# Gate logarithms, their chunk totals and the column-tiled products of a gated linear-attention and ternary feed-forward layer on Trainium2

## The reference

```python
xn = layernorm(x)
Q, K, V = xn @ Wq.T, xn @ Wk.T, xn @ Wv.T            # per head 16 wide
g     = max(sigmoid(xn_head @ gw.T), 1e-6)
log_c = clip(cumsum(log(g), axis=tokens), -30, 30)   # per head
Gc    = exp(log_c) + 1e-6
R     = silu(K @ sw.T)
S     = cumsum(K V^T * R / Gc, axis=tokens) * Gc     # a 16x16 state per head
attn  = (Q S) @ Wo.T
h     = bitlinear(xn, w_fc) + gate * (xn @ v.T @ fast_b.T @ u.T)    # ternary weights, 1024 hidden
ffn   = bitlinear(relu(h) ** 2, w_proj)
out   = x + attn + ffn
```

## Time and profile before

| | before |
|---|---|
| median of 3 runs | 652.83 us |
| profiled execution | 652.83 us |
| span of its profile | 651.0 us |
| PE busy | 629.2 us, 97% of the span |
| DVE, ACT, POOL busy | 507.5, 435.3, 357.1 us |
| granted TensorE clock, mean | 0.998 |
| chain that ended last | PE 92%, DMA 3%, SP queue 2% |

### The profile page before, as it was taken

One profiled execution on the slowest core, in us unless ns is written; L12 is line 12 of the kernel. 1 busy time (PEld: TensorE's weight loads), 2 busy tenths in 40 slices (PEclk: granted clock), 3 DMA queues, 4 the chain that ended last, 5 costly groups with the idle time before them and its releaser, 6 DMA issues.

```text
span 651.0 us, 21292 instructions
## 1 busy us (share of the span) xinstructions
PE 629.2 (97%) x7734; PEld 546.5 (84%) x7734; DVE 507.5 (78%) x1245; ACT 435.3 (67%) x999; POOL 357.1 (55%) x434
## 2 busy tenths in 40 slices
PE   3889999999999999999999999999999999999997
PEld 3668888888888888888888888888888888888886
DVE  5998888878787777877778877877787777878673
ACT  2688666767666776766677676667676666767662
POOL 4766465554555555456455555645555554655355
PEclk9999999999999999999999999999999999999999
DMA  9347755666746765554567856667656465677421
GB/s 309 94 124 121 111 140 135 148 142 131 111 117 129 138 132 139 135 119 112 130 139 136 143 130 97 132 136 129 143 130 135 106 125 128 141 128 127 100 45 34
DMA packets 186793, 83.05 MB, mean 128 GB/s; under 512 B 118320, under 2 KB 186160, under 8 KB 186688
## 3 DMA queue, kind: packets, MB, share of 16 engines
q1 hardware_dynamic: 184448, 79.05, 58.3%
q10 hardware_dynamic: 2240, 2.62, 1.2%
HBM read 12.43 MB, written 8.39 MB: 32 GB/s over the span
## 4 chain that ended last, share of the span: by engine, by line
PE 92%; DMA 3%; SPq 2%; DVE 1%; issue 1%; POOL 0%; POOLq 0%; DVEq 0%
PE y_bank L2251 17%; PE attn_bank L2195 9%; PE hid_b L2230 9%; PE hid_a L2230 9%; PE front_b L2132 7%; PE y_bank L2265 7%; PE front_a L2113 6%; PE front_b L2094 6%; PE score_a L2161 5%; PE attn_bank L2209 5%; PE score_b L2161 4%; PE attn_bank L2180 3%; PE hid_a L2232 2%; PE hid_b L2232 2%; DMA x_sb<-in_x 2%
## 5 line engine op out<-in xcount | busy, mean ns | idle before, releaser
L2251 PE MATMUL y_bank<-wproj_t,sq_h 128*128 128x256 f16 x512 | 118.5, 273 | 0.0
L2251 PE MATMUL y_bank<-wproj_t,sq_l 128*128 128x256 f16 x512 | 118.5, 273 | 0.0
L1727 DVE TENSOR_TENSOR sq_l<-relu_sq,sq_h 128x512 f16<-128x512 f32 x128 | 105.3, 824 | 1.0 <-ACT relu_sq L1032 0.9
L1680 DVE TENSOR_TENSOR masked<-score_a,shapes_sb 128x512 f32<-128x512 f32 x128 | 87.0, 680 | 16.0 <-PE score_a L2161 15.9
L1680 DVE TENSOR_TENSOR masked<-score_b,shapes_sb 128x512 f32<-128x512 f32 x128 | 87.2, 681 | 11.8 <-PE score_b L2161 11.7
L666 POOL TENSOR_TENSOR state_diag<-state,state_mask 128x256 f32<-128x256 f32 x56 | 53.4, 954 | 63.6 <-DVE state L1699 63.1
L1032 ACT ACTIVATE relu_sq<-relu_sq 128x512 f32<-128x512 f32 x128 | 79.6, 623 | 9.8 <-DVE sq_l L1727 9.7
L653 POOL COPY decay_halves<-decay 128x1024 uint16<-128x1024 uint16 x32 | 33.2, 1038 | 87.3 <-ACT decay L983 87.3
L697 POOL TENSOR_TENSOR y_both<-y_both,x_sb 128x512 f32<-128x512 f32 x32 | 41.2, 1287 | 70.0 <-DVE y_both L1739 70.0
L1023 ACT ACTIVATE sq_h<-relu_sq 128x512 f16<-128x512 f32 x128 | 79.2, 620 | 0.1
L933 ACT ACTIVATE vg<-front_b 128x304 f32<-128x304 f32 x64 | 27.2, 425 | 71.9 <-PE front_b L2132 71.8
(11 more groups left out here) (189 smaller groups left out, 1662.2 us busy)
## 6 DMA issues: line engine op xcount, KB each, us to landing
q_diag<-q SPq DMA_DIRECT2D x256, 64.0 KB, 2.7
k_stack<-k SPq DMA_DIRECT2D x128, 128.0 KB, 3.8
x_sb<-in_x SPq DMA_DIRECT2D x32, 256.0 KB, 3.3
out_y<-y_both SPq DMA_DIRECT2D x32, 256.0 KB, 3.4
relu_sq<-in_w_fc ACTq DMA_DIRECT2D x1, 1024.0 KB, 11.1
pj_nat<-in_w_proj ACTq DMA_DIRECT2D x1, 1024.0 KB, 13.8
y_both<-in_w_qk ACTq DMA_DIRECT2D x1, 512.0 KB, 4.6
w_stage<-in_w_qkvz_t SPq DMA_DIRECT2D x1, 512.0 KB, 6.3
```

The lines of the kernel that those rows point to most:

```text
L1680: nc.vector.tensor_tensor(masked[:, c, g].rearrange("p (h n) -> p h n", h=4), score_bank[g % 2][:].rearrange("p (h n) -> p h n", h=4), cau ...
L1727: nc.vector.tensor_tensor(sq_l[:, q], sq[:, n], sq_h[:, q], ALU.subtract).then_inc(sq_l_done, 1)
L2251: last = mm(y_bank[:, c * D:(c + 1) * D], part[:, q, at:at + P], wproj_t[:, 2 * q + i], start=(q == i == c == n == 0), stop=False, skip_gr ...
```

## The change

Seven things change.
1. The running sum is one fp16 product of 64 columns. The logarithm, times 1024, is taken as two fp16 parts (`log_high` on ACT, `log_low` on DVE); the sum of what stood before is no longer in the product.
2. DVE adds the two parts out of front_a at once (`sums_taken`), which frees that bank; `keys` waits for it and no longer for `clip_log`. The last row of that result, the totals of the two chunks, is copied from partition 127 to all partitions by a transfer of SP (`spread_totals`), and POOL adds them up (`sums_before`). `clip_log` becomes two instructions.
3. The two chunks' `values` and both `state_updates` stand in one block; the updates go to the second score bank, the values of both chunks to the four quarters of attn_bank. `chunk_out` (twice, 256 elements) becomes `unit_out` (once, 512).
4. `scores` (c, g) = (0, 1) waits until the state has been read out of that bank. `diagonal_state` waits for `carried` instead of DVE.
5. DVE's two small `tensor_scalar` in `dens` become `scalar_tensor_tensor` with a second tensor of constants.
6. All lists are reordered: `slot` of PE now has the values of u+2, the scores of u+3 and the queries of u+4. The setup's order changes too.
7. There is one slot less (LAST 29), and the last units stand in longer lists.

```diff
             def cumulate(b, u):
+                if first_of_all(b, u):
+                    pe.wait_ge(causal_made, 1)
                 pe.wait_ge(k16_l_done, upto(b, u, 1, 0))
-                pe.wait_ge(before_step, upto(b, u, 2, 0))
-                cum = front_a[:, 0:CH * H]
-                mm(cum, causal_sb, log_den[:].rearrange("p c h -> p (c h)"), start=True, stop=False)
-                mm(cum, ones[:], before[:, u % 2].rearrange("p c h -> p (c h)"), start=False,
+                pe.wait_ge(log_l_done, upto(b, u, 1, 0))
+                mm(front_a[:, 0:2 * CH * H], causal16[:], log16[:].rearrange("p s c h -> p (s c h)"), start=True,
                    stop=True).then_inc(cum_full, 1)
...
+            def log_high(b, u):
+                act.wait_ge(log_den_done, upto(b, u, 1, 0))
+                nc.scalar.activation(log16[:, 0], log_den[:], ACT.Copy, scale=LOG_SCALE).then_inc(log_h_done, 1)
...
+            def log_low(b, u):
+                dve.wait_ge(log_h_done, upto(b, u, 1, 0))
+                nc.vector.scalar_tensor_tensor(out=log16[:, 1], in0=log_den[:], scalar=LOG_SCALE, in1=log16[:, 0],
+                                               op0=ALU.mult, op1=ALU.subtract).then_inc(log_l_done, 1)
+
+            def sums_taken(b, u):
+                dve.wait_ge(cum_full, upto(b, u, 1, 0))
+                parts = front_a[:, 0:2 * CH * H].rearrange("p (s n) -> p n s", s=2)
+                nc.vector.tensor_reduce(chunk_sums[:, par].rearrange("p c h -> p (c h)"), parts, AX.X,
+                                        ALU.add).then_inc(sums_taken_done, 1)
...
+            def spread_totals(b, u):
+                sp.wait_ge(sums_taken_done, upto(b, u, 1, 0))
+                last = chunk_sums[P - 1:P, par].rearrange("p c h -> p (c h)")
+                sp.dma_start(totals[:, par].rearrange("p c h -> p (c h)"),
+                             last.unsqueeze(1).to_broadcast([1, P, CH * H])).then_inc(totals_spread[par], 16)
...
+            def sums_before(b, u):
+                pool.wait_ge(totals_spread[par], turned_upto(b, u))
+                nc.gpsimd.tensor_tensor(before[:, par, 1], before[:, par, 0], totals[:, par, 0],
+                                        ALU.add).then_inc(before_step, 1)
...
+                    nc.gpsimd.tensor_tensor(before[:, 1 - par, 0], before[:, par, 1], totals[:, par, 1],
+                                            ALU.add).then_inc(before_step, 1)
...
             def keys(b, u):
-                    pe.wait_ge(log_c_done, upto(pb, pu, 1, 0))
+                    pe.wait_ge(sums_taken_done, upto(pb, pu, 1, 0))
...
+            def state_updates(b, u):
+                pe.wait_ge(mask_done, upto(b, u, 4 * CH, 4 * CH - 1))
+                for c in range(CH if u < NU - 1 else CH - 1):
+                    for t in range(KT):
+                        for j in range(4):
+                            at = (c * KT + t) * P // 2
+                            last = mm(update_bank[32 * j:32 * j + 32, at:at + P // 2],
+                                      k_tok[:, par, c, t * P + 32 * j:t * P + 32 * j + 32],
+                                      v_lanes(par, c, t, j // 2), start=(c == t == 0), stop=True, skip_group_check=True)
+                last.then_inc(updates_done, 1)
...
             # scores
+                if (c, g) == (0, 1) and exists(pb):
+                    pe.wait_ge(state_done, states_upto(pb, pu, CH - 1 if pu < NU - 1 else 0))
...
             # PE slot, after
+                projected(*nxt, 2)
+                hidden(*after, 2)
+                values(*after, 0)
+                state_updates(*after)
+                values(*after, 1)
+                carried(*after, 0)
+                cumulate(*unit_after(b, u, 3))
+                queries_t(*unit_after(b, u, 4))
+                keys(*unit_after(b, u, 4))
+                scores(*unit_after(b, u, 3), 0, 0)
+                carried(*after, 1)
+                scores(*unit_after(b, u, 3), 0, 1)
...
             # SP slot, after
+                stack_queries(*unit_after(b, u, 3))
+                turn_keys(*unit_after(b, u, 3))
+                load(*unit_after(b, u, 6))
+                turn_tokens(*unit_after(b, u, 4))
+                stack_keys(*unit_after(b, u, 3))
+                turn_z(*unit_after(b, u, 3))
+                turn_decays(*after)
+                spread_totals(*unit_after(b, u, 3))
+                store(b, u)
...
             # DVE, setup
+                stats_of(0, 2)
+                gate_maxima()
                 scale_columns(1)
-                gate_maxima()
-                stats_of(0, 2)
                 columns_low(0)
```

More of the change, by code:

```diff
@@ new lines, in slot @@
+                sums_taken(*unit_after(b, u, 3))
+                scalars_of(*unit_after(b, u, 6))
+                squares_low(*after, 1)
+                carry_state(*after, 1)
+                squares_low(*after, 2)
+                mask(*unit_after(b, u, 3), 0, 0)
+                mask(*unit_after(b, u, 3), 0, 1)
+                queries_low(*unit_after(b, u, 4))
+                keys_low(*unit_after(b, u, 4))
+                mask(*unit_after(b, u, 3), 0, 2)
+                refine_rstd(*unit_after(b, u, 6))
@@ L1845, in prologue @@
-                carry_state(0, 0, 0)
+                squares_low(0, 0, 0)
+                projection_scale()
+                dens(0, 1)
+                output_inverse()
+                carry_state(0, 0, 0)
+                log_low(0, 1)
+                squares_low(0, 0, 1)
+                sums_taken(0, 1)
+                carry_state(0, 0, 1)
+                mask(0, 1, 0, 0)
+                squares_low(0, 0, 2)
+                queries_low(0, 2)
+                mask(0, 1, 0, 1)
+                mask(0, 1, 0, 2)
@@ new lines, in prologue @@
+                refine_rstd(1, 0)
+                queries_low(0, 3)
+                squares_low(0, 1, 2)
+                mask(0, 2, 0, 0)
+                scale_y(0, 0)
+                mask(0, 2, 0, 1)
+                clip_log(0, 2)
+                keys_low(0, 3)
+                mask(0, 2, 0, 2)
+                unit_out(0, 1)
+                mask(0, 2, 0, 3)
+                mask(0, 2, 1, 0)
+                z_low(0, 3)
+                squares_low(0, 1, 3)
+                write_factors(0, 2)
@@ L1940, in prologue @@
+                stats_of(1, 3)
+                z_low(1, 0)
+                log_low(1, 0)
+                carry_state(0, 3, 0)
                 waits_for_stats(1, 3)
                 moments_of(1, 3)
-                chunk_out(0, 3, 1)
+                squares_low(0, 3, 1)
+                sums_taken(1, 0)
+                scalars_of(1, 3)
+                carry_state(0, 3, 1)
+                mask(1, 0, 0, 0)
+                queries_low(1, 1)
+                unit_out(0, 3)
                 mask(1, 0, 0, 1)
+                refine_rstd(1, 3)
@@ new lines, in prologue @@
+                mask(1, 0, 1, 1)
+                mask(1, 0, 1, 2)
+                dens(1, 1)
+                mask(1, 0, 1, 3)
+                log_low(1, 1)
+                squares_low(1, 0, 0)
+                squares_low(1, 0, 1)
+                stats_of(2, 0)
+                z_low(1, 1)
+                carry_state(1, 0, 0)
+                sums_taken(1, 1)
+                squares_low(1, 0, 2)
+                carry_state(1, 0, 1)
+                mask(1, 1, 0, 0)
+                unit_out(1, 0)
@@ L1964, in epilogue @@
+                carry_state(7, 3, 1)
                 scale_y(7, 2)
[L1965 removed]
+                unit_out(7, 3)
                 squares_low(7, 3, 3)
[L1967 to L1968 removed]
                 scale_y(7, 3)
@@ L2400, in prologue @@
-                keys(1, 0)
-                state_update(0, 2, 1)
-                values(0, 2, 1)
+                hidden(0, 3, 0)
                 scores(0, 3, 0, 0)
```

1054 lines of the change are left out of this document (565 added, 489 removed).

## The result

The changed kernel takes 671.66 us (median of four runs, 668.54 to 673.88), the kernel before 652.88 beside it: ratio 1.028, 95% interval 1.024 to 1.033. The forecast was 639.3, faster. The profiled execution took 671.0, its span is 669.2.

The account below looks back on a forecast made before the run. PE was taken to bound the steady part. From 652.83, minus 7.4 (one block), minus 10.1 (running sum), plus 3.4 (setup), plus 0.6 (end) gave 639.3 us; range 635 to 649, the forecast's own range 636 to 643.

Parts of the forecast that it names:

- What has to stay hidden: Count of steps on other engines and transfers within a slot of 18.55 us; all had slack, k_stack 1.5, cost 0.
- The block: PE's two column-tiled blocks become one, saving 0.23 a unit, 7.4 us in all, with seams taken as 0.
- rival A: Each change of shape or bank inside the block drains, so it saves nothing: loses 7.4, 646.7 us, chance 0.10.
- The sum's product: The running sum's fp16 product of 64 columns on PE costs 0.08, bounds 0.03 to 0.11; running-sum saving 10.1 us.
- Hidden steps: Slack for keys 1.0, for the state chain 1.6 to 1.9; totals free; SP's queue fits, 17.35 of 18.55 taken.
- rival B: A new PE wait each unit, at keys with DVE behind its order: 9.6 us, 648.9, chance 0.10.
- The setup: Moved DVE steps delay the first scores by 2.1; with the second unit's keys, cost 3.4 us, bounds 0 to 7.
- The second unit's wait: In the setup, SP's list brings the second unit's keys 1.3 us late for its scores.
- The end: Behind the last carried state, unit_out and POOL steps take 4.1 against PE's 3.5: cost 0.6, bounds -0.5 and 2.
- Rival C: SP's queue becomes the bound through the totals' issue and two new waits: slower, 664.9 us, chance 0.08.

Follow-up runs that it names:

- run 4: Changed kernel with a third q_t buffer, queries_full ahead of keys on ACT, and queries_low ahead of the two masks on DVE: 645.57 us, ratio 0.988.
- run 9: Changed kernel with the third q_t buffer and queries_full ahead of keys, but queries_low left behind the masks: 657.92 us, ratio 1.009.
- run 11: Changed kernel with one swap in SP's slot, the turn of the tokens issued ahead of the load of x: 663.90 us, ratio 1.016.
- run 10: Kernel before with only DVE's queries_low moved behind squares_low and two masks: 654.77 us, ratio 1.0024.
- run 8: run 7 with seven x buffers and the load issued first in SP's slot, ahead of the queries' stacks: 642.78 us, ratio 0.985.
- run 6: Changed kernel with gate_maxima and scale_columns(1) put back ahead of stats_of(0, 2) in DVE's setup: 666.51 us, ratio 1.021.
- run 3: Changed kernel without the transfer of the totals; POOL adds each partition's own last sum, so gates' sums are wrong: 666.29 us, ratio 1.020.
- run 7: Changed kernel with the edits of run 4 and run 6 together: 644.18 us, ratio 0.988.
- run 1: Changed kernel with SP's slot reordered: turn of keys, stacks of queries, stacks of keys, load, turn of tokens: 753.14 us, ratio 1.152.
- run 2: Changed kernel with only the load and the turn of the tokens moved behind the stacks of keys in SP's slot: 784.61 us, ratio 1.200.
- run 5: Changed kernel with seven x buffers and SP's order load, turn of keys, turn of tokens, stacks of queries, stacks of keys: 682.07 us, ratio 1.044.
- run 12: run 10 with the load issued ahead of the turn of the tokens in SP's slot: 663.69 us, ratio 1.017.

## Why the prediction was wrong, step by step

**The step that failed** is the third line of "What has to stay hidden": "The fresh k_stack is needed at 7.6. SP would issue it by 2.3 and it lands in 3.8: slack 1.5." Counted as there, from the start of the slot (2.06 ahead of the block), SP has issued the last stack at 3.5 in the median of 26 units (2.6 to 4.7), 1.2 late, and its median landing is 4.5, 0.7 late: 1.9 together, more than the slack. In the unit shown the slot starts at 380.27, the issue ends at 3.2, and the scores start at 10.2 in place of 7.6.

The count was a chain inside one slot, and it is the last piece of a loop. I took SP's start for given. Before the change `queries_low` stood ahead of the masks, and SP began its stacks 0.6 us behind the unit's first scores (319.25 in rows 8, and for PE of that kernel):
```profile
318.66 0.38 PE L2161 MATMUL score_a<-q_diag,k_stack 128*128 128x256 f16 x2
```
In the changed order it begins 2.8 behind them (369.19 and 372.02): two masks stand ahead, and ACT's `queries_full` waits for a product behind the same scores. Runs 4 and 9 show both edges. Add to it:
- a shorter unit, 18.5 in place of 19.1, which the loop has to fit into;
- landings of 4.5 (up to 7.7) in place of 3.8 (up to 5.2), which I took from rows 9 although the order of the issues ahead changes. Run 11 shows that the swap of load and turn makes them late.

Run 10 shows that a start 2.3 behind the scores costs 1.6 us while units take 19.1, run 11 that earlier landings return 7.8 in the changed kernel, net of what the later load costs. How the 26 us divide beyond that I can't say, since each counts only from where the others leave no slack. For such a count each landing needs its spread too, since a loop at its limit loses the late ones and never gains them back.

**The account of the 18.2 us** in the profiled executions: PE's work -19.1 (run 8's units against rows 2: 76.35 - 73.97 = 2.38 for four, x 8), setup up to the first scores +4.3 (PE's waits for `log`, 1.6, and for ACT, 1.2 against 0.6, lie in it), scores' waits +29.4 with the 0.16 of each, end +0.4: 15.0. The clock near the end adds 1.7 (last section). The other 1.5 I haven't traced.

**The block.** Values 0.90, updates 0.45, values 0.98 (382.33 to 384.66), and 0.20 from L2417 where 0.11 is normal; in other units the same within 0.01. The forecast had 0.88, 0.44, 0.99 and 0.09 for the entry. Right; the seams cost 0.03 together, and rival A is out.

**The sum's product.** Over 25 units with whole records the next start follows by 0.03 in the median, 0.04 in the mean (the unit shown has the largest, 0.12). I took 0.08 "nearer to the load", and it was at my lower bound: 1.3 to 1.6 us better than forecast. The Trainium skill, TensorE: Matmul & The Clock Gate, was near with its floor of about 25 ns for up to 64 columns (Back-to-back issue gap): 30 ns measured. Its price for a load of 128 columns, 107 ns (LDWEIGHTS), isn't paid: the load of the next product is hidden although only 64 columns stand in front of it.

**Hidden steps.** `keys` has no wait for `sums_taken` (rival B out), the state chain none. The totals land in 3.0; POOL waits for them 10.6 us in 7, PE never. SP's queue does have room.

**The setup.** `group_sums` at 17.67 against 17.4 forecast: right. The first scores at 44.63 against 42.7, 4.3 later than rows 10; which of the steps between took the 1.9 more isn't shown. Part of it may be the clock: from 31.86 to 35.03 PE takes 3.17 us, at 0.66 granted, for six products of 304 columns and two groups of 4 records, which take 0.77 and twice 0.44 in the kernel before, 1.5 less. Run 6 gets 1.9 back with the gates ahead of the statistics. The second unit's wait I gave 1.3; it is 1.9:
```profile
44.63 0.38 PE L2343 MATMUL score_a<-q_diag,k_stack 128*128 128x256 f16 x2 [1.31 <-DMA k_stack<-k]
...
59.54 0.38 PE L2343 MATMUL score_a<-q_diag,k_stack 128*128 128x256 f16 x2 [1.89 <-issue]
```
**The end.** PE waits 0.41 for the last attention, forecast 0.6. Right.

**Rival C** had the place (the queue of transfers), the sign and nearly the time, 664.9, for the wrong reason: new waits that fill the queue. The queue's own waits for z and for the sums are 10.1 and 4.0 us over the whole run; run 3 took one of them away, with the transfer, and returned 5.4 us. Its chance of 0.08 was the mistake that follows from taking slack in a loop for slack in a slot.

So what failed was not the price of the work. The kernel forecast at 639.3 exists but for 3.5 us, as run 8; it needs another order on three engines.

## What to carry to other kernels

Before shortening a loop's unit, write down every chain that leads from an instruction to the same instruction one unit later, through in-order lists and transfers, and compare its length with the new period: slack that is measured inside a slot is not there if the start of the slot moves too. When steps on an engine are reordered, look what stands between a released bank and the step that starts the queue; here two masks of 0.66 us and one missing buffer, with late landings, were worth 26 us. And move a load in a shared queue only after finding who reads it first: 4.4 us later cost 113.

## What the runs showed that I had not expected

- **A landing depends on what is issued just ahead.** With a load of 256 KB and then a turn directly ahead of them, the stacks of keys land in 4.2 to 4.5 us (median, six kernels: changed, runs 3, 4, 6, 7, 9), and q1 is busy 66 to 68% of the span. With the two swapped, the load elsewhere, or a store between, they land in 3.6 to 3.9 (before, runs 1, 2, 5, 8, 10, 11, 12), at 50 to 62%. The spans differ, but in us it is the same: share times span is 424 to 444 us in the first six, 380 to 413 in the others. The bytes are the same, 79 to 80 MB, so the DMA engines are held longer by the same work. What holds them I can't tell from these records.
- **The clock fell once after a short wait.** Windows of the changed kernel near its end:
```profile
635.00:640.00 5.00, 2.96 (x26) 2.42 (x23) 3.77 (x6) 0.87 (x2) 2.59 (x3) 0.92 0.47 73
640.00:645.00 5.00, 5.00 (x35) 4.12 (x34) 1.99 (x3) 2.07 (x3) 0.27 (x2) 0.74 0.23 54
```
The scores at 637.82 had waited 2.04 us; behind that the granted clock is 0.92 and then 0.74, that is, part of the time at 1.2 GHz. Against full speed the two stretches lack 0.08 x 5 + 0.26 x 5 = 1.7 us of PE's time. But two waits that were longer, 2.13 ahead of 390.42 and 2.20 ahead of 545.60, are followed by 1.00. So a wait of 2 us can cost more than itself, and did in one of the 22 cases; what decides isn't shown. In run 2, which waits 4 to 5 us in each unit, the mean from 300 to 400 us is 0.91. In the setup, 30 to 35 us has 0.66, and the column can miss such a stretch: in run 6 the products of 304 columns stand 0.26 apart from 28.59 on, twice the usual 0.13, while 25 to 30 and 30 to 35 us both have 1.00.
- **Products of different shape share the tiles without a gap.** 32 records of 64 columns on quarters of the array stand 0.45 us long, 14 ns each, between two groups of 128 columns, with seams of 0.01 to 0.02.
